# DLRM tower: an eleventh looked-up table, gathers in a ring of eight units over chunk pairs, a reordered start of each pair

## The reference

```
e = stack([tbl_f[ids[:, f]] for f in range(26)], axis=1)      # (2048, 26, 128)
sd = einsum('bfd,bd->bf', e, dense)                           # 26 products
pairs = einsum('bfd,bgd->bfg', e, e)[:, iu, ju]               # 325 products
h = concatenate([dense, sd, pairs, dense], axis=1)            # 607 columns
h = maximum(h @ W_top1 + b_top1, 0)                           # 607 -> 512
h = maximum(h @ W_top2 + b_top2, 0)                           # 512 -> 256
y = h @ W_top3                                                # 256 -> 1
```

## Time and profile before

| | |
|---|---|
| Three executions, median (lowest to highest) | 394.58 us (387.96 to 397.21) |
| The profiled execution | 392.26 us |
| its span from the first to the last instruction | 390.5 us |
| PE matmul busy in the span | 332.9 us |
| ACT busy | 202.2 us |
| DVE busy | 190.3 us |
| POOL busy | 258.1 us |
| mean granted clock of PE, share of full speed | 0.955 |

### The profile page before, as it was taken

One profiled execution on the slowest core, in us unless ns is written; L12 is line 12 of the kernel. 1 busy time (PEld: TensorE's weight loads), 2 busy tenths in 40 slices (PEclk: granted clock), 3 DMA queues, 4 the chain that ended last, 5 costly groups with the idle time before them and its releaser, 6 DMA issues.

```text
span 390.5 us, 8070 instructions
## 1 busy us (share of the span) xinstructions
PE 332.9 (85%) x3328; PEld 283.2 (73%) x3328; DVE 190.3 (49%) x444; ACT 202.2 (52%) x260; POOL 258.1 (66%) x262
## 2 busy tenths in 40 slices
PE   0897978339799998979899998879899998988976
PEld 0775867228788886868788887768788886977865
DVE  1896964300379783330478883230378773312211
ACT  3487755704444855644545745643644765655311
POOL 6777777777777777777777777777777777400000
PEclk9999989859899999998999999998999999996999
DMA  6998483442246114352245115362245212330310
GB/s 160 241 243 207 121 246 84 118 128 54 51 110 169 50 48 145 92 157 55 57 110 164 51 51 140 89 166 54 51 99 146 83 50 69 79 88 2 76 50 1
DMA packets 46547, 40.56 MB, mean 104 GB/s; under 512 B 29815, under 2 KB 40559, under 8 KB 46512
## 3 DMA queue, kind: packets, MB, share of 16 engines
q1 hardware_dynamic: 38320, 23.26, 23.0%
q0 software_dynamic: 8192, 16.79, 16.4%
HBM read 34.28 MB, written 5.76 MB: 103 GB/s over the span
## 4 chain that ended last, share of the span: by engine, by line
PE 66%; DMA 10%; POOL 9%; SPq 6%; issue 5%; ACT 4%; DVE 1%; POOLq 0%; DVEq 0%
PE oh_ps L492 31%; PE dot_ps L510 16%; PE mlp_ps L531 11%; POOL rows L324 9%; PE tr_ps L476 5%; PE mlp_ps L540 4%; DMA dots_scratch<-dots 3%; ACT feat L349 3%; SPq L250 3%; DMA zt<-dots_scratch 3%; SPq L259 2%; DMA rows<-tbl_dram,idx_sb 1%; DMA dots_scratch<-rows 1%; DMA feat<-dots_scratch 1%; DVE dots L427 0%
## 5 line engine op out<-in xcount | busy, mean ns | idle before, releaser
L324 POOL DMA_INDIRECT rows<-tbl_dram,idx_sb x256 | 257.6, 1006 | 79.2 <-issue 76.2
L418 DVE TENSOR_SCALAR onehot<-ids_bc 125x512 fp32r<-125x512 int16 x320 | 128.1, 451 | 28.7 <-PE oh_ps L492 24.0
L492 PE MATMUL oh_ps<-onehot,table_hi 125*128 125x512 f32 x320 | 103.9, 406 | 11.3 <-DVE onehot L418 11.3
L492 PE MATMUL oh_ps<-onehot,table_lo 125*128 125x512 f32 x320 | 100.5, 396 | 0.0
L349 ACT ACTIVATE feat<-tr_ps 128x512 f32<-128x512 f32 x64 | 78.1, 1237 | 15.4 <-PE tr_ps L476 15.0
L355 ACT ACTIVATE feat<-oh_ps 128x512 f32<-128x512 f32 x40 | 48.8, 1219 | 64.4 <-PE oh_ps L492 64.4
L510 PE MATMUL dot_ps<-feat 128*54 128x52 f32 x2048 | 61.8, 221 | 15.8 <-ACT feat L349 12.8
L492 PEld LDWEIGHTS oh_ps<-onehot,table_hi 125*128 125x128 f32 x320 | 58.7, 192 | 22.2 <-issue 11.5
L510 PEld LDWEIGHTS dot_ps<-feat 128*54 128x54 f32 x2048 | 58.5, 137 | 20.6 <-ACT feat L349 14.7
L531 PE MATMUL mlp_ps<-zt,w_sb 117*128 117x256 f32 x224 | 57.2, 411 | 18.2 <-DMA zt<-dots_scratch 18.2
L492 PEld LDWEIGHTS oh_ps<-onehot,table_lo 125*128 125x128 f32 x320 | 61.2, 191 | 13.6
(11 more groups left out here) (24 smaller groups left out, 55.4 us busy)
## 6 DMA issues: line engine op xcount, KB each, us to landing
ids_bc<-ids_t_dram SPq DMA_DIRECT2D x40, 128.0 KB
dots_scratch<-dots SPq DMA_DIRECT2D x28, 175.5 KB
rows<-tbl_dram,idx_sb POOLq DMA_INDIRECT x256, 2.7
dots<-tbl_dram SPq DMA_DIRECT2D x5, 480.0 KB
zt<-dots_scratch SPq DMA_DIRECT2D x14, 117.0 KB
w_sb<-tbl_dram SPq DMA_DIRECT2D x3, 480.0 KB
dense_sb<-dense_f_dram SPq DMA_DIRECT2D x8, 128.0 KB, 2.6
zt<-dense_t_dram SPq DMA_DIRECT2D x7, 128.0 KB
```

The lines of the kernel that those rows point to most:

```text
L324: nc.gpsimd.indirect_dma_start(rows[:, g, t, :], None, tables[UNIT[u][k]], bass.IndirectOffsetOnAxis(ap=idx_sb[:, n % 2, g * TILES + t:g * ...
L418: last = nc.vector.tensor_scalar(onehot_part(m, part)[:, c, :], ids_bc[0:TP, m % IDSLOTS, :], float(part * PROWS + c), None, ALU.is_equal)
L492: last = nc.tensor.matmul(oh_ps[:, m % 2, :], table[0:TP, u, row * D:(row + 1) * D], onehot_part(m, part)[:, c, :], start=(table is table_ ...
```

## The change

Eleven features are looked up instead of ten, so fifteen are gathered. These make, for a pair of chunks, 7 units of two features for chunk n, one unit of the fifteenth feature (`ODD`) for both chunks, and 7 units for chunk n + 1. `rows` is now a ring of 8 units that runs on over the pairs (step `r` is the unit of this pair, `q` one left over from the pair before), with the same size as before. The copy of a lookup gets a step of its own, `c`. From the second pair on, two lookups stand ahead of the products `d`; their copies wait for the products of the chunk before, since they write to both chunks of `feat`. Layers 1 and 2 of the very first chunk move from the end of the first pair (`p`) into the second (`SECOND`, step `o`), behind its two first lookups. `zt` has two buffers. Room for this comes from a smaller scratch for the DMA descriptors (`dynamic_dma_scratch_size=4096`). Indices are loaded once a pair. The diff, cut to its core:

```diff
--- before.py
+++ after.py
-NO = 10
+NO = 11
...
-UNITS = len(GATHERED) // 2
-UNIT = [GATHERED[2 * u:2 * u + 2] for u in range(UNITS)]
-NR = 2 * UNITS
+ALONE = len(GATHERED) // 2
+UNITS = 2 * ALONE + 1
+UNIT = [GATHERED[2 * u:2 * u + 2] for u in range(ALONE)]
+ODD = GATHERED[-1]
+RING = 8
...
-FIRST = ("i0 s0 i1 s1 l0 i2 s2 a0 l1 i3 s3 a1 l2 i4 s4 a2 l3 i5 s5 a3 l4 s6 i6 a4 l5 s7 i7 a5 l6 s8 i8 a6 l7 s9 i9 "
-         "a7 f l8 l9 e0 e1 b0 e2 e3 e4 e5 b1 e6 e7 j0 b2 g j1 b3 j2 j3 p0 p1 b4 p2 p3 j4 b5 p4 b6 j5 b7")
-LOOK = ("d0 d1 d2 d3 d4 d5 d6 d7 l0 a0 l1 a1 l2 i6 l3 a2 i7 l4 a3 i8 l5 a4 i9 l6 a5 l7 a6 l8 f l9 a7 "
-        "e0 e1 e2 e3 b0 e4 e5 e6 e7 ")
-REST = "m0 j0 b1 m1 m2 g b2 m3 j1 m4 b3 j2 p0 p1 j3 b4 p2 p3 j4 b5 p4 j5 b6 b7"
-REST_LAST = "m0 b1 m1 m2 g b2 m3 m4 b3 b4 b5 b6 b7"
+FIRST = ("i0 s0 i1 s1 l0 c0 i2 s2 r0 l1 c1 i3 s3 r1 l2 c2 i4 s4 r2 l3 c3 i5 s5 r3 l4 c4 s6 i6 r4 l5 c5 s7 i7 "
+         "l6 c6 s8 i8 r5 l7 c7 s9 i9 r6 l8 c8 s10 i10 r7 f l9 c9 l10 c10 r8 e0 e1 j0 e2 e3 r9 j1 e4 e5 g j2 e6 e7 "
+         "r10 j3 j4 r11 j5")
+SECOND = "l0 l1 q12 o0 q13 o1 o2 q14 o3 o4 d0 d1 d2 d3 r0 d4 d5 d6 c0 d7 c1 r1 "
+THEN = "l0 r0 l1 r1 d0 d1 d2 d3 d4 d5 d6 c0 d7 c1 "
+LOOK = ("r2 l2 c2 l3 c3 i6 r3 l4 c4 i7 r4 l5 c5 i8 l6 c6 i9 r5 l7 c7 i10 r6 l8 c8 r7 f l9 c9 l10 c10 "
+        "e0 e1 e2 e3 r8 e4 e5 e6 e7 ")
+REST = "r9 m0 j0 m1 r10 g m2 j1 m3 r11 m4 j2 p0 r12 p1 j3 p2 r13 p3 j4 p4 r14 j5 "
+REST_LAST = "r9 m0 m1 r10 g m2 m3 r11 m4 r12 r13 r14 "
 TAIL = "d0 d1 d2 d3 d4 d5 d6 d7 o0 o1 o2 o3 o4 m0 m1 m2 m3 m4"
-ORDER = [FIRST] + [LOOK + REST] * (NPAIR - 2) + [LOOK + REST_LAST, TAIL]
+ORDER = [FIRST, SECOND + LOOK + REST, THEN + LOOK + REST, THEN + LOOK + REST_LAST, TAIL]
...
-        rows = sb("rows", [P, NR, TILES, D], fp32)
+        rows = sb("rows", [P, RING, 2, TILES, D], fp32)
...
-        zt = sb("zt", [P, ZC + 1, CH], fp32)
+        zt = sb("zt", [P, 2, ZC + 1, CH], fp32)
...
-            if u < 3 or u >= 8:
-                return dots[:, u % 8 * RPP * D:(u % 8 + 1) * RPP * D]
-            if u == 3:
-                return zt[:].rearrange("p c b -> p (c b)")
+            if u < 3 or u >= 9:
+                return dots[:, u % 9 * RPP * D:(u % 9 + 1) * RPP * D]
+            if u in (3, 8):
+                return zt[:, u // 8].rearrange("p c b -> p (c b)")
...
+        def unit_view(i):
+
+            u = i % UNITS
+            if u == ALONE:
+                return feat[:, :, :, ODD + 1]
+            return feat_view(int(u > ALONE), UNIT[u % (ALONE + 1)])
...
-            def load_idx(n):
-                sp.dma_start(idx_sb[:, n % 2, :], idx[n]).then_inc(idx_loaded[n % 2], DMA)
+            def load_idx(j):
+                if j >= 2:
+                    sp.wait_ge(transposed, (j - 1) * UNITS)
+                sp.dma_start(idx_sb[:, j % 2, :], idx[j]).then_inc(idx_loaded[j % 2], DMA)
...
-            def next_idx(n):
-                sp.wait_ge(transposed, (n + 1) * UNITS)
-                load_idx(n + 2)
...
-                if 0 < n < NCH - 1:
-                    sp.wait_ge(l1_done, N1 // P * n)
+                if 1 < n < NCH - 1:
+                    sp.wait_ge(l1_done, N1 // P * (n - 1))
...
                 if j < NPAIR - 1:
-                    next_idx(n)
                     for u in range(IDSLOTS):
                         load_ids(NO * (j + 1) + u)
                 make_z(n)
                 if j < NPAIR - 1:
                     load_dense(n + 2)
-                    next_idx(n + 1)
+                if j < NPAIR - 2:
+                    load_idx(j + 2)
...
-            for n in range(NCH):
-                pool.wait_ge(idx_loaded[n % 2], DMA * (n // 2 + 1))
-                for u in range(UNITS):
-                    if n:
-                        pool.wait_ge(transposed, (n - 1) * UNITS + u + 1)
+            for i in range(NPAIR * UNITS):
+                j, u = divmod(i, UNITS)
+                if u == 0:
+                    pool.wait_ge(idx_loaded[j % 2], DMA * (j // 2 + 1))
+                if i >= RING:
+                    pool.wait_ge(transposed, i - RING + 1)
...
             def looked_up_to_feat(m):
                 act.wait_ge(onehot_read, PARTS * (m + 1))
+                if m >= NO:
+                    act.wait_ge(dots_done, 2 * (m // NO) * GUNITS)
...
                 if j:
+                    for i in range(PLACES, 2 * PARTS):
+                        make_part(NO * j + i // PARTS, i % PARTS)
+                    if j == 1:
+                        layer3(0)
                     dots_to_sbuf(n - 1)
-                    for i in range(PLACES, PARTS * NO):
+                    for i in range(2 * PARTS, NO * PARTS):
                         make_part(NO * j + i // PARTS, i % PARTS)
...
-                    pe.wait_ge(transposed_out, UNITS * (n + 1))
+                    pe.wait_ge(transposed_out, UNITS * ((n + 1) // 2) + (ALONE + 1) * ((n + 1) % 2))
...
-    nc = bacc.Bacc("TRN2", target_bir_lowering=False, num_devices=1)
+    nc = bacc.Bacc("TRN2", target_bir_lowering=False, num_devices=1, dynamic_dma_scratch_size=4096)
```

More of the change, by code:

```diff
@@ L143, in dlrm_tower @@
         ids_loaded = [sem(f"ids_loaded{s}") for s in range(IDSLOTS)]
-        rows_loaded = [sem(f"rows_loaded{u}") for u in range(UNITS)]
+        rows_loaded = [sem(f"rows_loaded{s}") for s in range(RING)]
         dense_loaded = sem("dense_loaded")
@@ L164, in dlrm_tower @@
         dots_stored = sem("dots_stored")
-        z_loaded = sem("z_loaded")
-        last_z_loaded = sem("last_z_loaded")
+        z_loaded = [sem(f"z_loaded{p}") for p in range(2)]
         l1_done = sem("l1_done")
@@ L234, in load_table @@
                 sp.dma_start(raw[120:TP], src[120:TP]).then_inc(table_loaded[u], DMA)
[L236 to L238 removed]
             def make_z(n):
                 z = z_of(n)
[L242 removed]
+                loaded = z_loaded[n % 2]
                 sp.wait_ge(dots_out_act, GUNITS * (n + 1))
@@ L276, in _ @@
             load_idx(1)
-            load_table(8)
-            load_table(9)
+            for u in range(8, NO):
+                load_table(u)
             for u in range(IDSLOTS, NO):
@@ L314, in _ @@
             nc.gpsimd.iota(diag, [[1, P]], base=0, channel_multiplier=-1).then_inc(iotas_made, 1)
[L316 to L328 removed]
+            for i in range(NPAIR * UNITS):
[4 more added lines that the diff above has]
+                    pool.wait_ge(transposed, i - RING + 1)
+                for k in range(2):
+                    f = ODD if u == ALONE else UNIT[u % (ALONE + 1)][k]
+                    for t in range(TILES):
+                        x = (2 * u + k) * TILES + t
+                        nc.gpsimd.indirect_dma_start(
+                            rows[:, i % RING, k, t, :], None, tables[f],
+                            bass.IndirectOffsetOnAxis(ap=idx_sb[:, j % 2, x:x + 1], axis=0),
+                        ).then_inc(rows_loaded[i % RING], DMA)
         @block.scalar
@@ L466, in _, with transposes @@
         def _(pe):
-            def transposes(n, u):
-                i = n * UNITS + u
-                pe.wait_ge(rows_loaded[u], DMA * TILES * 2 * (n + 1))
+            def transposes(i):
+                pe.wait_ge(rows_loaded[i % RING], DMA * TILES * 2 * (i // RING + 1))
                 if i == 0:
@@ L475, in transposes @@
                     for t in range(TILES):
-                        last = nc.tensor.transpose(tr_ps[:, i % 2, k, t * P:(t + 1) * P], rows[:, 2 * u + k, t, :],
+                        last = nc.tensor.transpose(tr_ps[:, i % 2, k, t * P:(t + 1) * P], rows[:, i % RING, k, t, :],
                                                    ident[:])
@@ L517, in layer1 @@
                 if x == 0:
-                    if n < NCH - 1:
-                        pe.wait_ge(z_loaded, DMA * Z_DMAS * (n + 1))
-                    else:
-                        pe.wait_ge(last_z_loaded, DMA * Z_DMAS)
+                    pe.wait_ge(z_loaded[n % 2], DMA * Z_DMAS * (n // 2 + 1))
                     if n == 0:
@@ L576, in grouped, with rows_of @@
         return a.reshape(Q, QS, -1).transpose(1, 0, 2).reshape(CH, -1)
-    idx = np.stack([grouped(ids[n * CH:(n + 1) * CH, GATHERED]).reshape(TILES, P, NR).transpose(1, 2, 0)
-                    for n in range(NCH)])
+    def rows_of(n, fs):
+        return grouped(ids[n * CH:(n + 1) * CH, fs]).reshape(TILES, P, -1).transpose(1, 2, 0).reshape(P, -1)
+    idx = np.stack([np.concatenate([rows_of(n, GATHERED[:-1]), rows_of(n, [ODD]), rows_of(n + 1, [ODD]),
+                                    rows_of(n + 1, GATHERED[:-1])], 1) for n in range(0, NCH, 2)])
     looked_up = np.stack([grouped(ids16[n * CH:(n + 1) * CH, ONEHOT]).T for n in range(NCH)])
```

48 lines of the change are left out of this document (22 added, 26 removed).

## The result

| | before | after |
|---|---|---|
| Median of 21 executions (lowest to highest) | 393.12 us (386.92 to 398.88) | 395.06 us (391.38 to 403.23) |
| Ratio to before, 95% interval | | 1.014 (1.010 to 1.018) |
| The profiled execution, its span | 392.26, 390.5 us | 403.23, 401.3 us |
| PE, DVE, ACT, POOL busy | 332.9, 190.3, 202.2, 258.1 us | 351.5, 201.3, 205.0, 245.1 us |

The change makes the kernel 1.4% slower, some 5.4 us; the forecast was 0.6%, and no difference by more than 2%. The ratio compares only the fast executions of the two kernels; the medians of all 21 are 1.9 us, 0.5%, apart, so the size of the loss is known less well than its direction. The profiled execution of the changed kernel is the slowest of its 21, so its span is not to be set against that of before as it stands; what it shows are places.

What follows compares the result with a forecast made beforehand. The prediction took PE's order, with holes, as the bound. Its terms, -4.4 + 5.3 (late ids) + 1.3 (clock), gave +2.2 us: 394.5 against the profiled execution, 397 with the median's 2.3 us, range 388 to 404.

Steps and rivals of the forecast that it cites:

- the ids' hole: New PE wait before l6 in pairs 1 to 3, behind late ids of feature 6; 3.3 to 7.4 us, 5.3 taken.
- D: Mark along PE: the end of products d7, where a pair's lookups begin; 110.41 us in pair 1 before.
- T: Mark along PE: the end of the last transposes of a pair; 188.95 us in pair 1 before.
- The first product and the first z: First pair: first product +0.3 us, at 62.3; hole before first layer 1 shrinks to some 5 us, layer at 85.3.
- The lookups and the leading pair: Two lookups ahead of products d: D to T -4.5 us; T to D +6.7 in pair 2, +6.3 in pair 3.
- one clock drop of 1.3: PE at a lower granted clock behind a hole of over two us: one taken, +1.3 us, between none and two.
- The argument for the lower end: POOL's pauses let ids land in 2.6 us like the dense vectors; holes before l6 then 3.3 us in all.
- my second rival: All of the ids' hole, each hole lowering the clock: +5.6 to +7 us, up to +9; 400 to 404; chance 0.22.
- my own +2.2: Own case, the holes before l6 partly there: -4.4 + 5.3 + 1.3 us; 393 to 401 us; chance 0.44.
- PE's order, with holes: Bound claimed for the whole kernel: PE's work counts in full, and what fills a PE hole is free.
- The rival of the gathers: POOL's gathers were the bound after all: 16 fewer save 21 us, giving 374 us; chance 0.07.
- The second z buffer: Removes a wait of SP that ended before the stores had landed; given nothing, up to 0.5 us of gain.

Runs made afterwards that it cites:

- first_back: Changed kernel with the layers of chunk 0 put back to the end of the first pair; 402.37 us, ratio to before 1.031.
- ids_early_3: Changed kernel with SP loading the ids of features 6 and 7 ahead of the z of chunk n - 1; 385.87 us, ratio to before 0.987.
- ten_ids_early_2: Changed kernel with ten lookups, sixteen gathered features and the ids of features 6 and 7 loaded early; 382.65 us, ratio to before 0.981.
- fill_z: ids_early with the next pair's first lookup moved into the hole before the layers of chunk n, in pairs 1 and 2; 379.50 us, ratio to before 0.970.
- lead_back: Changed kernel with the two leading lookups put back behind d7, ids still late; 391.41 us, ratio to before 1.004.
- after_again: Changed kernel unaltered, on a chip where before took 519.61 us; 504.59 us, ratio to before 0.972.
- ids_early: Changed kernel with ids of features 6 and 7 loaded ahead of the z of chunk n - 1, on a 500 us chip; 499.30 us, ratio to before 0.960.
- ids_early_2: The kernel of ids_early once more, on the second 500 us chip; 499.28 us against 524.53 for before, ratio 0.955.

## Why the prediction was right, step by step

The marks of the prediction (without the ids' hole) beside the profile of the changed kernel, us:

| | before | predicted | after |
|---|---|---|---|
| first layer 1 of chunk 0 | 84.86 | 85.3 | 87.52 |
| D of pair 1 | 110.41 | 107.6 | 109.8 |
| T of pair 1 | 188.95 | 181.7 | 187.4 |
| T of pair 2 | 277.56 | 272.5 | 282.9 |
| first product of the tail | 354.45 | 350.1 | 363.5 |

**The first product and the first z.** The first product came at 63.38 instead of 62.3, and PE waited 0.98 and 0.39 us more among the eight groups, the longer one for nothing that the profile names. I had put 0.2 us of ACT's work there; so the first layer 1 is 2.2 us late. The hole, 5.22 us, was right. From there to D it is 22.3 us, 22.25 in the sum, but by luck in part: the layers took 14.4 us (13.75 in the sum), beginning at the lower clock (0.50 from 87.52 to 91.30), and the products 7.9 (8.5), as DVE's layer 3 delayed them less. first_back bears out the worth of the move, 6.7 us.

**The lookups and the leading pair.** T to D of pairs 2 and 3 is 15.5 us twice (15.8 in the sum), no hole before the products, 0.98 us before l2 (1.2). Pair 2 was 90.85 in the sum without the ids' hole; ids_early_3 has 89.5 and 89.7.

**The ids.** The step that decided the sign, the two lookups spent ahead of D while i6 stays behind the z, was right in place, cause and order of size: 2.7, 1.7, 3.0 at most and 0.7, 0.8, 1.9 at least were given, 1.80, 2.46 and 1.75 measured. The mis-sized term is this one with its clock: I took the middle, 5.3 us, plus one clock drop of 1.3. The profile has 6.0 and two drops of 1.7, and ids_early_3 puts all of it at 10.6 us (8 to 13). The argument for the lower end, that POOL's pauses would let the ids land in 2.6 us, was wrong: in pair 2 they took from 215.30 to 219.7, 4.4 us, longer than before. And 2.6 us is the time of another load: over the whole changed kernel the loads of ids took 3.1 us at the least and 3.8 in the median, the dense vectors 2.6 in the median. In pair 3 the hole was ended by DVE's one-hot parts and not by ACT's copy, but they waited for the same shift. Had I taken the rows' own values and two drops, the sum would have been +5.6, and the ratio gives +5.4: that lies at the lower end of my second rival (chance 0.22), nearer to it than to my own +2.2. By the medians of all executions it is +1.9, so the time alone does not choose between the two; the holes of the profile speak for the rival. That 397 came within 2 us of 395.06 is luck in part: it stands on a median of three for before, 394.58, and that of 21 is 393.12.

**The layers and the tail.** Two more differences of the profile are in no term of the sum. The hole before the layers of chunk n and the lower clock behind it cost 1.8 us more than before in pair 1 (2.65 against 2.29 us, and 1.5 us of clock) and about as much in pair 2. And the tail, to which I gave nothing, takes 37.8 us instead of 36.1. This is its last layer 1 (timeline of PE), after:

```profile
385.94 8.87 PE L547 MATMUL mlp_ps<-feat,w_sb 117*128 117x256 f32 x32 [3.29 <-DMA feat<-dots_scratch]
```

and before:

```profile
376.79 7.19 PE L531 MATMUL mlp_ps<-feat,w_sb 117*128 117x256 f32 x32 [2.54 <-DMA feat<-dots_scratch]
```

The hole before the last layer 1 is 0.75 us longer and the 32 matmuls behind it begin at the lower clock (0.68 from 385.94 to 389.0), where before they took 7.19 us at 1.00; the products at the start of the tail are 0.6 us shorter (8.6 us at 363.47, 9.2 at 354.45). These terms are part of the 10.8 us between the two spans. How much of them is left in a usual execution no profile shows.

**What bounds the kernel.** "PE's order, with holes" held for before and after: the changed kernel waits 3.3 us for rows in all. The rival of the gathers was right to be kept, but as a limit a few us behind PE, not as the one that sets the time; ten_ids_early_2 ran into it. A sum along PE is good only while it stays above POOL's 1.3 us times the gathers.

**The rest.** The second z buffer was given nothing. That was not tried alone. SP's wait for layer 1 at this place went from 7.7 to 2.4 us, but behind it SP waits for the stores both times (8.0 and 13.3 us), as the prediction said. The share of the 8 us by which the profiled execution lies above the median that is the clock's, and what lowers it in one execution and not in another, stays open.

## What to carry to other kernels

Whoever moves work ahead of a wait takes it from behind another: count for each in-order queue how much cover the next blocking step (here one shift of ids) loses, and move its DMA as well. When two engines run side by side, give the second limit its own sum before you take work off the first. And a hole on PE may cost more than its length (the one of 2.46 us in the changed kernel was followed by a lookup that took 1.7 us longer), so the cheapest filler is work that is already waiting, put in front of the late step.

## What the runs showed of the hardware

**A hole and the clock.** In the changed kernel a hole of 1.75 us before l6 was followed by the lower clock in pair 3 (0.68 over the lookup), one of 1.80 in pair 1 was not (1.00); 2.46 in pair 2 was (0.69). Before the layers of chunk n, holes of 2.79 and 3.02 us in ids_early_3 were followed by eight matmuls in 2.65 and 3.59 us at granted clocks of 0.73 and 0.53, where eight take 1.9 at 1.00 (fill_z, 169.94); in lead_back one of 2.93 was followed by 1.00:

```profile
176.88 2.00 PE L545 MATMUL mlp_ps<-zt,w_sb 117*128 117x256 f32 x8 [2.93 <-DMA zt<-dots_scratch]
```

And in first_back one of 1.99 us was followed by 0.59 (3.22 us for eight, 271.48). The length of the hole alone does not tell.

**The two chips at 500 us.** There the gathers came at their usual interval (in after_again 0.30 us between two and 1.01 us each), but PE issued at times one or a few matmuls every 0.7 us for some 10 us on end, its weight loads at the same sparse pace, and waited for nothing that the profile names. DVE stood still for up to 13.5 us meanwhile, released by nothing that the profile knows (timeline of PE, then of DVE, in after_again):

```profile
380.04 0.35 PE L529 MATMUL dot_ps<-feat 128*54 128x52 f32 x3 [1.01 <-issue]
...
381.49 0.24 PE L529 MATMUL dot_ps<-feat 128*54 128x52 f32 x1 [1.09 <-issue]
```

```profile
371.53 0.76 DVE L433 TENSOR_SCALAR onehot<-ids_bc 125x512 fp32r<-125x512 int16 x2 [0.59 <-PE oh_ps L511]
...
385.79 1.10 DVE L442 COPY dots<-dot_ps 54x416 f32<-54x416 f32 x2 [13.49 <-remote]
```

The places are nearly the same in two programs of equal orders on the same chip (376 to 387 us in after_again, 377 to 388 in ids_early), and in ids_early_2 on the other chip it is 381 to 388, so they seem to go with the program. The kernels with fewer gathers (240 instead of 256) took less time there (504.59 and 499.30 us against 512.69, 509.02 and, for before, 519.61). Whether the gathers have to do with it nothing was run to show; POOL waited 99.7 us for places in `rows` in after_again, so it was not the limit there. The cause stays open.
